# Attention 0 of a two-layer decoder: 24 steps of two row groups in place of 48 slots of one, and values once per batch

## The reference

```python
q, k, v = silu(x @ Wq), silu(x @ Wk), silu(x @ Wv)      # 16 heads of 16 features
D = exp(ld[h] * max(i - j, 0)) * (i >= j)                 # decay of head h
scores = einsum('bchd,bshd->bhcs', q, k) * D
o = einsum('bhcs,bshd->bchd', scores, v)
o = o * sigmoid(gate);  o = o * rsqrt(mean(o*o per head) + eps) * norm_w
x = x + o @ Wo
```

## Time and profile before

| | |
|---|---|
| runs | 1037.66, 1042.09, 1042.62 us |
| profiled execution | 1034.71 us, its span 1032.9 us |
| granted clock, mean | 0.967 |
| PE busy | 947.3 us (92%) |
| DVE busy | 633.0 us (61%) |
| ACT busy | 437.7 us (42%) |
| slots of attention 0 | from 50.7 to 120.6 us |
| first matmul of the experts after the last norm | 139.56 us |

### The profile page before, as it was taken

One profiled execution on the slowest core, in us unless ns is written; L12 is line 12 of the kernel. 1 busy time (PEld: TensorE's weight loads), 2 busy tenths in 40 slices (PEclk: granted clock), 3 DMA queues, 4 the chain that ended last, 5 costly groups with the idle time before them and its releaser, 6 DMA issues.

```text
span 1032.9 us, 14127 instructions
## 1 busy us (share of the span) xinstructions
PE 947.3 (92%) x5344; PEld 735.2 (71%) x5344; DVE 633.0 (61%) x1222; ACT 437.7 (42%) x1036; POOL 113.8 (11%) x126
## 2 busy tenths in 40 slices
PE   5999779999999988888788999999998799999998
PEld 4666457888888777656476777777775578888886
DVE  4357655666566553455566867868776456666664
ACT  4722443433334313666534444434444533334432
POOL 1300000000000046000031322222221000000000
PEclk9989869999999989988999999999999899999999
DMA  5000031111110040000060000000000312111101
GB/s 215 1 2 1 1 109 46 46 51 56 46 30 1 0 163 1 2 1 2 1 275 1 2 1 1 2 1 1 2 1 1 122 33 62 47 46 46 30 1 41
DMA packets 12089, 38.37 MB, mean 37 GB/s; under 512 B 1888, under 2 KB 3968, under 8 KB 11136
## 3 DMA queue, kind: packets, MB, share of 16 engines
q1 hardware_dynamic: 12000, 37.60, 10.7%
q0 software_dynamic: 32, 0.01, 0.0%
HBM read 36.55 MB, written 1.05 MB: 36 GB/s over the span
## 4 chain that ended last, share of the span: by engine, by line
PE 73%; ACT 8%; DVE 5%; issue 1%; POOL 0%; DVEq 0%
PE ps L1005 68%; ACT Q L840 3%; PE ps L1455 2%; PE ps L1110 1%; DVE nm L482 1%; ACT probs_q L917 1%; ACT whi L855 1%; DVE stats L384 1%; DVE X L589 1%; ACT L874 0%; ACT silu_g L874 0%; ACT L917 0%; PE ps L1243 0%; PE ps L1135 0%; DVE rope_buf L649 0%
## 5 line engine op out<-in xcount | busy, mean ns | idle before, releaser
L879 ACT ACTIVATE h_hi<-weighted_h 128x512 fp32r<-128x512 f32 x100 | 63.2, 632 | 152.3 <-DVE weighted_h L575 152.3
L1005 PE MATMUL ps<-xTh,whi 128*128 128x512 f32 x400 | 125.2, 394 | 2.2 <-ACT silu_g L874 2.2
L1005 PE MATMUL ps<-xTh,wlo 128*128 128x512 f32 x400 | 123.9, 391 | 0.0
L1005 PE MATMUL ps<-xTl,whi 128*128 128x512 f32 x400 | 123.2, 389 | 0.0
L577 DVE TENSOR_TENSOR h_lo<-weighted_h,h_hi 128x512 fp32r<-128x512 f32 x100 | 69.3, 693 | 69.8 <-ACT h_hi L879 69.8
L572 DVE TENSOR_TENSOR shared_gate<-silu_g,row_shares 128x512 f32<-128x512 f32 x88 | 60.9, 692 | 64.7 <-ACT silu_g L874 64.6
L1005 PE MATMUL ps<-xT,merged_q 128*128 128x256 f32 x384 | 92.4, 384 | 1.7 <-DVE rope_buf L650 1.7
L874 ACT ACTIVATE silu_g<-ps 128x512 f32<-128x512 f32 x100 | 59.6, 596 | 79.2 <-PE ps L1005 78.9
L1005 PEld LDWEIGHTS ps<-xTh,whi 128*128 128x128 f32 x400 | 74.5, 189 | 21.5 <-issue 5.5
L997 POOL TENSOR_TENSOR latent_rot<-rope_buf 128x256 f32<-128x256 f32 x96 | 68.6, 736 | 190.7 <-DVE rope_buf L650 190.7
L1005 PEld LDWEIGHTS ps<-xTh,wlo 128*128 128x128 f32 x400 | 75.7, 189 | 15.9
(11 more groups left out here) (181 smaller groups left out, 1639.4 us busy)
## 6 DMA issues: line engine op xcount, KB each, us to landing
raw<-in_ffn SPq DMA_DIRECT2D x50, 384.0 KB, 3.1
wx<-in_wx SPq DMA_DIRECT2D x4, 2048.0 KB, 10.0
cx<-in_cx SPq DMA_DIRECT2D x1, 1536.0 KB, 9.7
wqkv<-in_wqkv SPq DMA_DIRECT2D x1, 1280.0 KB, 10.4
X<-in_x SPq DMA_DIRECT2D x4, 256.0 KB, 3.5
rope_buf<-in_kvc SPq DMA_DIRECT2D x1, 1024.0 KB, 4.7
out<-X SPq DMA_DIRECT2D x4, 256.0 KB, 2.3
cst<-in_const SPq DMA_DIRECT2D x1, 773.0 KB, 7.8
```

Of the source, the lines that this page charges most:

```text
L879: a.activation(h_hi[:, u % 2, :], weighted_h[:, u % 2, :], ACT.Copy).then_inc(act_hi[l], 1)
L1005: return pe.matmul(o, l, r, start=start, stop=stop, skip_group_check=True)
```

## The change

Attention 0 gets 24 steps (3 per half batch) in place of 48 slots. A step n fills two banks with the scores of two row groups, whose matmuls alternate; step k = 0 of a half has the 128 x 128 part (P1) of four heads in each bank, k = 1 and 2 the 256 queries (P0) of two. The two pairs of banks take turns, so step n waits for the product of step n-2. `decayed(n)` is one product of 128 x 1024. The values of a batch are computed once all six of its products are done, on four column groups, in four quarters (first and last keys, two blocks m of features), and each quarter stands behind one step of the next batch. P0 and P1 have two halves by b % 2 now, as in attention 1. The tests that place og, scaled, add_out, normalise and bilinear are written anew.

```diff
+            def decayed(n):
+
                 v.wait_ge(pe_s, n + 1)
...
+                if k == 0:
+                    v.tensor_tensor(P1[:, b % 2, 8 * half:8 * half + 8, :], step_scores(n).rearrange("p i (h q) -> p (i h) q", h=4),
+                                    DT[:, 8 * half:8 * half + 8, 0:128], ALU.mult).then_inc(p_done, 1)
                 else:
...
+                    v.tensor_tensor(by_group(P0, b, half, k - 1), step_scores(n).rearrange("p i (e q) -> p i e q", e=2),
+                                    DT[:, 8 * half:8 * half + 8, :].rearrange("p (i m e) q -> p i m e q", i=2, m=2)[:, :, k - 1], ALU.mult).then_inc(p_done, 1)
...
-                for u in range(HALVES + 2):
...
+                for turn in range(HALVES + 5):
+                    for k in range(3):
+                        n = 3 * turn + k
+                        if n < STEPS:
+                            decayed(n)
+                        b = (turn - 3) // 2
+                        if (turn % 2, k) == (1, 2) and 0 <= b < NB:
+                            v.wait_ge(pe_o, b + 1)
...
-                        if (u % 2, j) == (1, 0):
+                        if (turn % 2, k) == (0, 2) and 0 <= b < NB:
                             scaled(0, b)
...
-            def mixed_values(u):
...
+            def mixed_values(b, quarter):
+
+                st, m = divmod(quarter, 2)
+                if quarter == 0:
+                    pe.wait_ge(p_done, 6 * b + 6)
...
+                    if b >= 2:
+                        pe.wait_ge(x_part, 2 * (b - 1))
+                for e in range(2):
+                    for g in range(4):
+                        last = mm(ps[32 * g:32 * g + 32, value_bank(0, b), 256 * m + 128 * st:256 * m + 256], value_weights(2 * b + st, m, g, e),
+                                  (P0 if st == 0 else P1)[:, b % 2, 4 * g + 2 * m + e, :], st + m + e == 0, st + e == 2)
...
+            def scores_by_key(n):
 
                 b, half, k = n // 6, n // 3 % 2, n % 3
                 if n >= 2:
-                    pe.wait_ge(p_done, DECAYED + n - 1)
+                    pe.wait_ge(p_done, n - 1)
+                heads = 4 if k == 0 else 2
...
+                for h in range(heads):
+                    m, e = divmod(h, 2) if k == 0 else (k - 1, h)
+                    kk = (kE, kO)[e]
+                    for i in range(2):
+                        r = slice(64 * half + 32 * i, 64 * half + 32 * i + 32)
...
+                            if n < 2:
                                 pe.wait_ge(gate_ready, NB)
+                            scores_by_key(n)
+                        b = turn // 2 - 1
+                        if turn % 2 == 0 and k >= 1 and 0 <= b < NB:
+                            mixed_values(b, k - 1)
+                        if turn % 2 and k <= 1 and 0 <= b < NB:
+                            mixed_values(b, k + 2)
+                        if (turn % 2, k) == (0, 0) and 1 <= b <= NB:
+                            pe.wait_ge(sq_ready, b)
+                            mm(ps[:, value_bank(0, b - 1), :], block_ones, sq[:, :], True, True).then_inc(pe_ss, 1)
+                        if (turn % 2, k) == (1, 0) and 1 <= b <= NB:
+                            output(0, b - 1)
```

More of the change, by code:

```diff
@@ L274, in by_group @@
             return tile[:, b % 2, 8 * half:8 * half + 8, :].rearrange("p (i m e) q -> p i m e q", i=2, m=2)[:, :, m]
-        def decayed_of(tile, u):
-            return tile[:, 0, 8 * (u % 2):8 * (u % 2) + 8, :].rearrange("p (j e) q -> p j e q", e=2)
         def value_bank(l, b):
@@ L760, in decay @@
                 for h in heads:
-                    a.activation(DT[:, h, :], k("dist"), ACT.Exp, scale=ld_bc[:, h:h + 1]).then_inc(dt_exp, 1)
+                    a.activation(DT[:, 4 * (h // 2 % 4) + 2 * (h // 8) + h % 2, :], k("dist"), ACT.Exp, scale=ld_bc[:, h:h + 1]).then_inc(dt_exp, 1)
             def transposed_tokens(i, b):
@@ L1039, in gate @@
                 last.then_inc(pe_gate, 1)
-            def mixed_values(u):
-                b = u // 2
-                for st in range(2):
-                    for m in range(2):
-                        for e in range(2):
-                            for gi in range(2):
-                                g = 2 * (u % 2) + gi
-                                last = mm(ps[32 * g:32 * g + 32, value_bank(0, b), 256 * m + 128 * st:256 * m + 256], value_weights(2 * b + st, m, g, e),
-                                          decayed_of(P0 if st == 0 else P1, u)[:, 2 * m + gi, e, :], st + m + e == 0, st + e == 2)
-                last.then_inc(pe_o, 1)
+            def mixed_values(b, quarter):
+                st, m = divmod(quarter, 2)
+                if quarter == 0:
+                    pe.wait_ge(p_done, 6 * b + 6)
+                    pe.wait_ge(v_ready, 2 * b + 2)
+                    if b == 0:
+                        pe.wait_ge(k_ready, 2 * NB)
+                    if b >= 2:
[4 more added lines that the diff above has]
+                                  (P0 if st == 0 else P1)[:, b % 2, 4 * g + 2 * m + e, :], st + m + e == 0, st + e == 2)
+                if quarter == 3:
+                    last.then_inc(pe_o, 1)
             def output(l, b):
@@ new lines, in attention0 @@
+                for turn in range(HALVES + 5):
+                    for k in range(3):
+                        n = 3 * turn + k
+                        if n < STEPS:
+                            if n % 6 == 0:
+                                pe.wait_ge(q_ready, turn // 2 + 1)
+                                pe.wait_ge(k_ready, 2 * (turn // 2) + 2)
+                            if n < 2:
+                                pe.wait_ge(gate_ready, NB)
+                            scores_by_key(n)
[4 more added lines that the diff above has]
+                            mixed_values(b, k + 2)
+                        if (turn % 2, k) == (0, 0) and 1 <= b <= NB:
+                            pe.wait_ge(sq_ready, b)
+                            mm(ps[:, value_bank(0, b - 1), :], block_ones, sq[:, :], True, True).then_inc(pe_ss, 1)
+                        if (turn % 2, k) == (1, 0) and 1 <= b <= NB:
+                            output(0, b - 1)
```

93 lines of the change are left out of this document (19 added, 74 removed).

## The result

The changed kernel takes 1048.14 us (median of 5 runs, 1046.62 to 1049.48), the kernel before beside it 1040.88 us (5 runs). The ratio is 1.0074, with a 95% interval from 1.0046 to 1.0103: slower by 5 to 11 us, where 10 us less was forecast. The runs of the kernel before are spread over 7 us (1035.29 to 1042.62), the longer ones at a lower mean clock (of the 19 beside the first experiments those near 1035.5 us have 0.965, those near 1042 us 0.955 to 0.957). The profiled execution of the changed kernel took 1046.62 us, its span is 1044.8 us, its mean granted clock 0.937 (before: 0.967). In the changed kernel the helper of the matmuls is L989, the products are L460 and L463, og L495, on L432, add_out L441, `xn` L385, sq L771.

The account below looks back on a forecast made before the run. The loop was taken as bound by the handover of scores from PE to DVE. Loop 19.2 us less, tail 6.0 more, 13.1 at the last `xn`, less 3.1 for low clock: gain 10.0, from 1042.1 to 1032.1 us, range 1024 to 1040.

Parts of the forecast that it names:

- The products: DVE in attention 0: 24 products of 128x1024 at 1.23 us each, 1.15 us per step with overlap.
- The order and its sizes at the upper clock: Attention 0 laid out batch by batch: last product ends at 101.4 us, last `xn` starts at 126.0 instead of 139.09.
- The gain of the loop: Attention 0's loop: last product ends at 101.4 us instead of 120.6, a gain of 19.2 us.
- Two side sums: Lower bound of a product, 1.07 us from columns alone; drain at six extra turns per batch, some 3 us later.
- the rule on the drain: Quarters on PE: changing the tiling mode drains TensorE; at six extra turns per batch, some 3 us later.
- The tail in the changed kernel itself: After the last product: two chains follow one another, 24.5 us to the last `xn` against 18.5 before.
- The quarters: Values on PE in attention 0: 3.0 us per batch, no quarter holding PE longer than 1 us.
- I leave this stretch low: First batch of attention 0: clock 0.51 from 53 to 60 us as before, its steps taking some 9.3 us.
- I put 3.1 us for both: Two more low clock stretches, in attention 0's loop and tail, cost 3.1 us together.
- The falsifier named for it: Clock in attention 0: the prediction would be wrong if low stretches after 60 us summed to over 20 us.
- more of the clock is lost: Attention 0's loop and tail: three low stretches and a low tail leave a gain of 3 to 5 us, 1038 us; chance 0.15.
- The rival on the handover and tail: Attention 0: banks two steps ahead keep the loop at 68.8 us, start and tail add 6.9, 1049 us; chance 0.07.

Follow-up runs that it names:

- the last run: Changed kernel with one added matmul in each of the first six steps, others at the waits and the end, against the kernel before: 1020.52 us, ratio 0.9829.
- the two kernels with added matmuls: Changed kernel with one added matmul per step and filled waits, 1027.05 us; kernel before with the same (one per two slots), 1039.2 us.

## Why the prediction was wrong

The forecast was 1032.1 us, range 1024 to 1040. Step by step:

- The products: 1.23 us each was worked out, 1.22 was measured. Right.
- The order and its sizes at the upper clock: right. The first products of the second, third and fourth batch were laid out at 62.0, 71.7 and 87.6 us, the end of the last product at 101.4 and the last `xn` at 126.0. With the clock kept up and no added matmuls behind the sixth step but for the waits and the end, they are at 61.72, 72.17, 88.14, 101.92 and 125.03 us. The first of these agrees by luck: it was laid out with a low stretch, and the run had none, but it had a later first product (53.57 for 52.7) and six added matmuls. The tail took 23.1 us, 24.5 were laid out.
- The gain of the loop, 19.2 us, was reckoned from the kernel before as it is, with its low stretches (120.6 us); so reckoned the last run gives 18.7. That the two kernels with added matmuls lie 19.0 apart is a coincidence, since these cost the kernel before more. The tail costs 6.6 us there (6.0 was worked out).
- Two side sums are off, without bearing on the forecast. At 1.07 ns a column 1024 columns are 1.10 us, not the 1.07 given as the lower bound of a product. And six turns of 0.33 us per batch, less the 0.3 counted, make 1.7 us and over three batches 5 us, not 3; the rule on the drain was not needed, since a step and its quarter take 2.06 us at the upper clock (61.82 to 63.88 in the last run), as laid out.
- The tail in the changed kernel itself: from the end of the last product (125.63) to the last `xn` 26.0 us, 24.5 were laid out (24.6 as rounded to 126.0). The last two og stand 10.4 us apart, 10 were. Right, but for an output and sums at the lower clock.
- The quarters: no quarter holds PE over 1.1 us at the upper level. Right. At the lower level one takes 1.94 us.
- The step that failed is the clock, that is, the term for low stretches in the sum. "I leave this stretch low: PE was full and the start is the same", three or four steps at 2 us and the rest at 1.1 to 1.2, took it as given that the clock comes back at 60 us as before. And for all further stretches, "I put 3.1 us for both". It did not come back until 97.0 us: of the 68.3 us from 52.6 to 120.9, all but 6.8 were low. From the laid-out 126.0 to 151.64 us is 25.6 us, where 3.1 stood. Batch by batch against the layout: the first is 1.3 us late (63.34 for 62.0), the second takes 17.2 us in place of 9.7, the third 23.3 in place of 15.9, the fourth 21.8 in place of 13.8, the tail 1.5 more. So the price of a slow first batch was about right; what was missing is that the batches with quarters would run at the lower clock too, where a step and its quarter hold PE 3.87 us. The falsifier named for it, low stretches after 60 us of over 20 us, was the one that came true (54 us up to 120.9), and with it the last product after 110 us and DVE's waits over 15 us.
- The rival "more of the clock is lost" had the mechanism and a chance of 0.15, but took three stretches at 2 to 3 us each and so 1038 us. Its price per stretch was read from the kernel before, where a low stretch ends in a pass of values after 7 us. The change removes that pass: the first values come behind the eighth step, one pass per batch remains, and it is cut up. The runs with slots and with steps show that values once a batch lengthen the low stretch from 6.8 to 17 us and the quarters from there to 44 us. A price from a row holds only while what ended the row's state is still there.
- The rival on the handover and tail gave 1049 us, near the result, by another mechanism. Where the values come twice a batch in one piece its mechanism shows (6.25 us per half batch at the upper clock, 6.51 before), but in the changed kernel the loop at the upper clock runs as laid out, so the near number is luck.
- By the Trainium skill, "TensorE: Matmul & The Clock Gate", part 1, the clock is gated down by idleness. The prediction weighed that for the tail only. The runs here agree for the tail (the last output 1.99 us with PE kept at work, 3.78 without), and do not in the loop: PE is shown busy 19.26 of 20 us with the clock at 0.50.
- What stays open: what makes the clock fall in one execution and not in another at the same work, and whether rows, pauses or the number of passes decide.

## What to carry to other kernels

Before cutting up or shortening matmul work, look at what raised the clock in the rows before, and price the case that it does not rise: a lower clock is a state that lasts, not a fixed toll. If a change that should gain loses and the granted clock differs, run both kernels with the clock held up by idle matmuls; that shows whether the clock is the cause. For the change's own worth count what the added matmuls cost each kernel, which is more where PE has no idle time left to take them. In the end few may be needed: here those in the first six steps, at the waits and at the end. A moved wait on one engine's queue (ACT here) can take back what the other engine gained.

## What the runs showed of the hardware

- A busy PE is not an upper clock. With scores on 32 rows and quarters of values PE showed 19.26 of 20 us busy (60 to 80 us) and stayed at the lower level for 44 us.
- The state can last: steps with quarters ran at 1.00 from 62 to 101 us when they began at the upper level (with sq's waits filled), and at 0.50 from 62 to 93 us when they began at the lower (waits not filled). It need not: with the waits filled they lost the upper level at 96.9 us in one execution.
- With values twice a batch the clock from 53 to 120.9 us was 0.90 (slots) and 0.80 (steps), with values once a batch in one piece 0.63 (slots) and 0.65 (steps), in one execution each; over whole runs the averages are 0.960, 0.952, 0.946 and 0.945.
- One bf16 matmul of 128 rows and 512 columns among the six steps of scores kept the clock at 1.00, with the waits filled; one of 32 rows in its place, which runs beside the scores, did not (0.51 from 60 to 80 us; one of its 12 runs, at 1023.02 us and a mean clock of 0.971, is likely an exception). Two of 128 rows per step without the waits filled did not raise it before 82.2 us.
